# Dense products ahead of TensorE's first wait in eight stages, and score products on quarters of the array in a local attention

## The reference, cut to what matters

```
DIM = 128; HEADS = 8; DIM_HEAD = 64; WINDOW = 64; QK_SCALE = 8.0
def local_attention(q, k, v):
    b, h, n, d = q.shape
    w = n // WINDOW
    bq = q.reshape(b, h, w, WINDOW, d) * QK_SCALE
    bk = k.reshape(b, h, w, WINDOW, d)
    bv = v.reshape(b, h, w, WINDOW, d)
    bk, bv = (look_around(bk), look_around(bv))
    sim = jnp.einsum('bhwid,bhwjd->bhwij', bq, bk)
    mask = (i < j) | (i > j + WINDOW) | (j == -1)
    sim = jnp.where(mask, -jnp.finfo(sim.dtype).max, sim)
    attn = jax.nn.softmax(sim, axis=-1)
    out = jnp.einsum('bhwij,bhwjd->bhwid', attn, bv)
    return out.reshape(b, h, n, d)
...
o = local_attention(q, k, v)
x = x + o @ wo
```

## Time and profile before

| | us |
|---|---|
| median of 3 runs | 4181.39 |
| lowest and highest of them | 4177.72, 4183.64 |
| profiled execution, its own time | 4167.43 |
| its span, first to last instruction | 4165.7 |

### The profile page before, as it was taken

One profiled execution on the slowest core, in us unless ns is written; L12 is line 12 of the kernel. 1 busy time (PEld: TensorE's weight loads), 2 busy tenths in 40 slices (PEclk: granted clock), 3 DMA queues, 4 the chain that ended last, 5 costly groups with the idle time before them and its releaser, 6 DMA issues. The chain is left out here.

```text
span 4165.7 us, 87048 instructions
## 1 busy us (share of the span) xinstructions
PE 3015.8 (72%) x34526; PEld 2091.1 (50%) x34526; DVE 2557.0 (61%) x7026; ACT 1448.0 (35%) x2873; POOL 787.8 (19%) x759
## 2 busy tenths in 40 slices
PE   4567887886547788788554778878856477787885
PEld 3434565654434456565443445656535244565653
DVE  6674565557676456555757745764575764566457
ACT  4134433422404344342240434434224044343421
POOL 3132211101213221110121322121012132111110
PEclk7579999997657899899765889999976588999996
DMA  1011000000001100000000110000000011000000
GB/s 37 6 38 30 14 3 2 14 20 1 7 6 38 30 14 3 2 14 20 1 7 6 40 30 12 3 2 18 16 1 7 6 40 30 11 3 2 19 14 6
DMA packets 65264, 59.65 MB, mean 14 GB/s; under 512 B 16403, under 2 KB 54212, under 8 KB 64838
## 3 DMA queue, kind: packets, MB, share of 16 engines
q1 hardware_dynamic: 63606, 53.24, 4.7%
q10 hardware_dynamic: 1232, 0.61, 0.1%
HBM read 36.29 MB, written 2.10 MB: 9 GB/s over the span
## 5 line engine op out<-in xcount | busy, mean ns | idle before, releaser
L157 POOL TENSOR_TENSOR ln_rstd<-ln_var_eps,neghalf 128x4 f32<-128x4 f32 x128 | 130.1, 1017 | 1223.6 <-DVE ln_var_eps L169 1188.5
L1188 POOL TENSOR_TENSOR l1t_ss<-l1t_ss,neghalf 128x16 f32<-128x16 f32 x64 | 243.7, 3808 | 478.8 <-DVE l1t_ss L1222 478.8
L2103 ACT ACTIVATE l2r_P<-l2r_bank_score 128x512 f32<-128x512 f32 x320 | 173.7, 594 | 176.3 <-PE l2r_bank_score L1825 176.3
L2103 ACT ACTIVATE l2a_P<-l2a_bank_score 128x512 f32<-128x512 f32 x320 | 173.7, 594 | 168.7 <-PE l2a_bank_score L1825 168.7
L1395 PE MATMUL l1t_ring<-l1f_qkv,x_normT 128*128 128x512 f32 x384 | 218.8, 699 | 13.1 <-ACT x_normT L1095 13.1
L1995 DVE CUSTOM_DVE_ANT_0 l2r_masked<-l2r_bank_ring,l2r_neg_wide 128x512 bf16<-128x512 f32 (+1 forms) x256 | 148.7, 622 | 76.7 <-PE l2r_bank_ring L1794 76.4
L1995 DVE CUSTOM_DVE_ANT_0 l2a_masked<-l2a_bank_ring,l2a_neg_wide 128x512 bf16<-128x512 f32 (+1 forms) x256 | 149.0, 622 | 73.9 <-PE l2a_bank_ring L1794 72.6
L1825 PE MATMUL l2a_bank_score<-l2a_q_head,l2a_k_head 32*128 32x128 f32 x2560 | 188.3, 284 | 2.4 <-DMA l2a_q_head<-l2a_shiftT 1.0
L1794 PE MATMUL l2r_bank_ring<-l2r_k_head,l2r_q_head 32*128 32x128 f32 x2432 | 174.6, 286 | 19.9 <-DVE l2r_m L1995 9.8
L1794 PE MATMUL l2a_bank_ring<-l2a_k_head,l2a_q_head 32*128 32x128 f32 x2432 | 176.7, 286 | 16.4 <-DVE l2a_m L1995 7.1
L1825 PE MATMUL l2r_bank_score<-l2r_q_head,l2r_k_head 32*128 32x128 f32 x2560 | 186.0, 282 | 2.6 <-DMA l2r_q_head<-l2r_shiftT 1.2
(11 more groups left out here) (616 smaller groups left out, 7949.6 us busy)
## 6 DMA issues: line engine op xcount, KB each, us to landing
l1t_v_low<-l1t_v SPq DMA_DIRECT2D x112, 130.0 KB, 2.3
l2e_w<-in_L_ffn_w SPq DMA_DIRECT2D x96, 128.0 KB, 2.3
l1f_qkv<-in_L_ffn_wqkv SPq DMA_DIRECT2D x8, 768.0 KB, 4.5
l1f_tables<-in_l_tables SPq DMA_DIRECT2D x8, 512.0 KB, 6.0
l1f_w<-in_L_ffn_w SPq DMA_DIRECT2D x8, 341.0 KB
x_in<-in_L_attn_hidden_states SPq DMA_DIRECT2D x10, 256.0 KB, 3.5
l1f_wo<-in_L_ffn_wo SPq DMA_DIRECT2D x8, 256.0 KB, 4.8
l2a_q_head<-l2a_shiftT SPq DMA_DIRECT2D x128, 2.0 KB
```

The source lines that it names most:

```text
L157: pool.tensor_tensor(b.rs[:, p, :], b.ve[:, p, :], b.neghalf[:, 0:NT], ALU.pow).then_inc(s["post_rstd"] if post else s["pre_rstd"], 1)
L1188: pool.tensor_tensor(ss[:, n % 2], ss[:, n % 2], b.neghalf[:, 0:2 * H8], ALU.pow).then_inc(s["rn_ready"], 1)
L2103: act.activation(self.P[:, use % self.P_RING].rearrange("k h q -> k (h q)"), self.score_bank(h, g)[:, :], ACT.Exp, scale=self.scale).then_ ...
```

## The change

**Dense products.** A new function `busy` issues `count` bfloat16 products of 128x512, the identity times a mask, into a bank that the stage overwrites later. It stands as the first thing in TensorE's program in eight blocks, ahead of `transpose_x` and its wait: 20 in l0_ffn, 10 in l1_attn, 10 in the local attention at depth 0, 10 in l2_attn, 20 in l2_ffn_attention, 10 in the experts, 10 in l3_attn, 20 in l3_ffn. They feed nothing.

**Score products.** `scores(n)` now writes the masks and then 24 q·k products: for each chunk, the 64 keys of the tile's first block against all 128 queries, into partitions 0 to 63 of the bank; the 64 keys of the block before against the first 64 queries and those of the second block against the last 64, into partitions 64 to 127. So each product uses 64 rows and 64 columns of the array. The order of keys in the banks changes with it: `neg_k` is built anew, and the two halves of `v_low` change places. For the first tile of a sequence POOL clears the upper half of `v_low` instead of the lower, with a settle before and after.

**Order.** The products with the shift are a function of their own, `subtract(n)`, with the wait for L1338 ahead. `scores(n + 1)` is issued after the projection of v and before `turn_output(n - 1)`, and no longer waits for the shift.

The programs of VectorE, ScalarE and SP keep their order.

```
+def busy(pe, b, bank, count):
+    for _ in range(count):
+        pe.matmul(bank[:, :], b.ident_bf[:], b.neg["row_gt"][:].unsqueeze(1).to_broadcast([128, 4, 128]),
+                  start=True, stop=True)
...
+            busy(pe, b, y[1], 20)                      # l0_ffn
             transpose_x(pe, b, s["xq_ready"], s["xT_psum"], xq, bank)
...
+            busy(pe, b, at.ring[0], 20)                # l2_ffn_attention
             transpose_x(pe, b, s["h_ready"], s["hT_psum"], h, at.y)
...
     for first, m in enumerate(w.neg_k):
-        keep(m[:], [[0, 2], [-1, 64]], 0, 1, fill=MASKED)
-        keep(m[:], [[0, 2], [1, 64]], 64, -1, fill=MASKED)
-        if first:
-            keep(m[:, 0:64], [[0, 64]], -64, 1, fill=MASKED)
+        keep(m[:, 64:128], [[-1, 64]], 0, 1, fill=MASKED)
+        keep(m[:, 64:128], [[1, 64]], 64, -1, fill=MASKED)
+        keep(m[:, 0:64], [[1, 64]], 0, -1, fill=MASKED)
+        if not first:
+            own.settle()
+            own(pool.tensor_copy(m[64:128, 0:64], w.neg_low[64:128, 0:64]))
...
-                sync.dma_start(v_low[64:128, p, j], v[0:64, p, j]).then_inc(s["v_low_ready"], 16)
+                sync.dma_start(v_low[0:64, p, j], v[0:64, p, j]).then_inc(s["v_low_ready"], 16)
                 if j:
-                    sync.dma_start(v_low[0:64, p, j], v[64:128, p, j - 1]).then_inc(s["v_low_ready"], 16)
+                    sync.dma_start(v_low[64:128, p, j], v[64:128, p, j - 1]).then_inc(s["v_low_ready"], 16)
...
-            own(pool.memset(v_low[0:64, :, 0], 0.0))
+            own.settle()
+            own(pool.memset(v_low[64:128, :, 0], 0.0))
+            own.settle()
...
             def scores(n):
                 j, p = tiles[n]
-                pe.wait_ge(s["q_ready"], n + 1)
-                pe.wait_ge(s["k_ready"], n + 1)
-                pe.wait_ge(s["shiftT_ready"], n + 1)
                 if n:
                     pe.wait_ge(s["p_ready"], 2 * n)
...
+                pe.wait_ge(s["q_ready"], n + 1)
+                pe.wait_ge(s["k_ready"], n + 1)
+                for c in range(CHUNKS):
+                    at = 128 * c
+                    for half, here, keys, queries in ((0, 0, j * 128 + 64, slice(0, 128)), (1, 0, j * 128, slice(0, 64)),
+                                                      (1, 64, j * 128 + 128, slice(64, 128))):
+                        for u in range(2):
+                            rows = slice(64 * u, 64 * u + 64)
+                            pe.matmul(s_bank[u][64 * half:64 * half + 64, at + here:at + queries.stop],
+                                      k[rows, p, c, keys:keys + 64], q[rows, n % 2, c, queries], start=False, stop=True,
+                                      skip_group_check=True)
+
+            def subtract(n):
+                p = tiles[n][1]
+                pe.wait_ge(s["shiftT_ready"], n + 1)
                 for u in range(2):
                     for c in range(CHUNKS):
-                        pe.matmul(s_bank[u][:, c * 128:(c + 1) * 128], w.sel[:, 4 * u + c, :], shiftT[:, p, :],
-                                  start=False, stop=True, skip_group_check=True)
...
+                        last = pe.matmul(s_bank[u][:, c * 128:(c + 1) * 128], w.sel[:, 4 * u + c, :], shiftT[:, p, :],
+                                         start=False, stop=True, skip_group_check=True)
+                    last.then_inc(s["s_ready"], 1)
...
+            scores(0)
             turn_shift(0)
             for n in range(T):
-                scores(n)
+                subtract(n)
...
                 if n + 3 < T:
                     project(n + 3, "v")
+                if n + 1 < T:
+                    scores(n + 1)
                 if n:
                     turn_output(n - 1)
```

More of the change, by code:

```diff
@@ L965, in _ @@
         def _(pe):
+            busy(pe, b, k_ps[0], 10)
             transpose_x(pe, b, s["xn_ready"], s["xT_psum"], b.xn, y)
@@ L1031, in l1_ffn_constants @@
         own(pool.tensor_copy(m[64:128, :], w.neg_low[64:128, :]))
+    own.settle()
+    own(pool.memset(w.neg_low[:], 0.0))
+    keep(w.neg_low[:, 0:64], [[-1, 64]], -64, 1, fill=MASKED)
     for first, m in enumerate(w.neg_k):
-        keep(m[:], [[0, 2], [-1, 64]], 0, 1, fill=MASKED)
-        keep(m[:], [[0, 2], [1, 64]], 64, -1, fill=MASKED)
-        if first:
-            keep(m[:, 0:64], [[0, 64]], -64, 1, fill=MASKED)
+        keep(m[:, 64:128], [[-1, 64]], 0, 1, fill=MASKED)
[4 more added lines that the diff above has]
+            own(pool.tensor_copy(m[64:128, 0:64], w.neg_low[64:128, 0:64]))
     keep(w.sel[:], [[-1, H8], [0, 128]], 0, 1, ALU.not_equal, 1.0)
@@ L1374, in _ @@
             if d == 0:
+                busy(pe, b, y[1], 10)
                 transpose_x(pe, b, s["xn_ready"], s["xT_psum"], b.xn, y)
@@ L1475, in scores @@
                               start=True, stop=True, skip_group_check=True)
+                pe.wait_ge(s["q_ready"], n + 1)
[12 more added lines that the diff above has]
+                pe.wait_ge(s["shiftT_ready"], n + 1)
                 for u in range(2):
                     for c in range(CHUNKS):
-                        pe.matmul(s_bank[u][:, c * 128:(c + 1) * 128], w.sel[:, 4 * u + c, :], shiftT[:, p, :],
-                                  start=False, stop=True, skip_group_check=True)
-                for c in range(CHUNKS):
-                    for blk in range(2):
-                        keys, at = j * 128 + 64 * blk, 128 * c + 64 * blk
-                        for u in range(2):
-                            rows = slice(64 * u, 64 * u + 64)
-                            last = pe.matmul(s_bank[u][:, at:at + 64], k[rows, p, c, keys:keys + 128],
-                                             q[rows, n % 2, c, 64 * blk:64 * blk + 64], start=False, stop=True,
-                                             skip_group_check=True)
-                            if (c, blk) == (CHUNKS - 1, 1):
-                                last.then_inc(s["s_ready"], 1)
+                        last = pe.matmul(s_bank[u][:, c * 128:(c + 1) * 128], w.sel[:, 4 * u + c, :], shiftT[:, p, :],
+                                         start=False, stop=True, skip_group_check=True)
+                    last.then_inc(s["s_ready"], 1)
             project(0)
@@ L2489, in _ @@
         def _(pe):
+            busy(pe, b, out[0], 10)
             transpose_x(pe, b, s["t_ready"], s["xT_psum"], t, turned)
@@ L2713, in _ @@
         def _(pe):
+            busy(pe, b, ring[3], 10)
             transpose_x(pe, b, s["xn_ready"], s["xT_psum"], b.xn, ring)
@@ L2921, in _ @@
         def _(pe):
+            busy(pe, b, g_ps[0], 20)
             transpose_x(pe, b, s["xq_ready"], s["xT_psum"], xq, t_ps)
```

## The result

The changed kernel takes 4054.5 us (median of 4 runs, 4051.5 to 4056.6). Beside it the kernel before takes 4182.5 us (4177.7 to 4191.5). The ratio is 0.969, with a 95% interval from 0.967 to 0.971. The forecast was 4118, with a range from 4075 to 4158: the direction was right, and the gain was twice the one forecast.

What follows compares the result with a forecast made beforehand. TensorE was taken to bound the local attention. Score products -47, order -15, clock +14 and dense products -15 sum to -63 us: 4104 for the profiled run, 4118 as median, range 4075 to 4158.

Steps and rivals of the forecast that it cites:

- What bounds: Local attention tile: TensorE sets the time, so each nanosecond it saves counts until VectorE's 2.58 us of slack is gone.
- The score products: q·k in each local attention tile: 1.93 us falls to 1.2, saving 47 us over 64 tiles (37 to 68).
- the ends 0.87 to 1.35: Bounds in us for a tile's q·k: 0.87 if quarters never idle, 1.35 at the pace of the values' records.
- The maxima's row: Profile row of sixteen bfloat16 records on four quarters, 22 ns each; at that rate 48 records take 1.05 us.
- The float32 row: Profile row of the values' float32 products on array halves, records 28 ns apart; at that rate 48 take 1.35 us.
- The place in the order: Local attention: issuing the next tile's scores earlier fills no wait in steady tiles, only at pass starts: 15 us (8 to 18).
- The starts of the passes: First two tiles of each local attention pass: earlier scores fill waits, 1.9 us for each of eight passes, 15 us.
- The clock in the local attention: More clock falls expected in the eight passes, 3.5 us each: 14 us more than now (14 less to 36 more).
- The stage starts: Dense products ahead of stages' first waits raise the clock for real products: 15 us gained (0 to 30).
- The step from the profile to the median: Whole kernel: the median before lies 14 us above the profiled run, so 4104 becomes a forecast median of 4118.
- the second, no loss of clock: Rival for the local attention: clock falls stay or vanish and l2_ffn_attention is always warm; 4063 to 4098 us, chance 0.22.
- the strict order: Rival for q·k: records start only in program order, 1.7 us a tile, gain 15 us, total 4150; chance 0.13.

## Why the prediction was wrong

By its own steps:

- **What bounds.** Right. Each 0.1 us that TensorE lost in a tile came off the pass, and VectorE's slack was not used up: in the tile shown it still idles for 2.1 of 10.92 us.
- **The score products.** 1.10 us, inside the ends 0.87 to 1.35 and below the 1.2 taken. I had averaged two rows. The maxima's row, of the same shape of tile, gave 22 ns a record; the new ones take 1.10 / 48 = 23 ns. The float32 row, on halves, was the wrong one to average in. 54 us instead of 47.
- **The place in the order.** "Moving it saves nothing unless it fills a wait" failed. The move changed what stands behind the wait, and 0.26 of its 0.56 us was the restart and not ScalarE; 0.20 of that went. 64 x 0.20 = 13 us that the sum did not have. The row that shows it was in the trace of before: the copy of the shift ends 0.26 us ahead of the mask. The starts of the passes were right: about 2 us each, 17 in all, for the 15 forecast.
- **The clock in the local attention.** Forecast 14 us more, measured about none. Steady terms give 54 + 13 + 17 = 84, and the two depths gained 83.6. The falls inside passes went from five to seven, but at some 1.6 us each where they had cost 2.8: in depth 1, two falls took 107.0 - 103.9 = 3.1 us. The forecast of more falls was right and its price was not: I gave each of the eight passes 3.5 us, from the old falls, and two of those had kept the clock low for 10 us at a time, as here in turn 2 of the kernel before:

```profile
1305.00:1314.00 9.00, 9.00 (x52) 6.95 (x52) 3.98 (x6) 3.82 (x7) 3.81 (x1) 0.50 0.04 9
```

The larger price of the clock, at the beginning of a pass, was in none of my terms; it did not make the forecast wrong, since the change left it there.
- **The stage starts.** 15 us forecast, 28 measured. Right: l0_ffn and l3_ffn next to nothing at 20 products, l1_attn 0.8 for nothing, l2_attn 4.3 for 6, though unevenly (1.7 us in turns 1 and 4, 0.4 in turns 2 and 3). Mis-sized: l3_attn, 2.7 us a turn for the 0.75 forecast. The earlier rise is worth 1.4 us, the difference between the two turns without a second fall (59.9 before, 58.5 after). The rest is that second fall, some 19 us into the stage. It came in three turns of four before and cost 2.5 to 3.1 us, and in two after, at 1.8. Wrong in its reason: l2_ffn_attention gained the whole 9 us, and it does so without its dense products too. That this term came out at all is luck: the trace of before happened to hold one slow turn, the second one two.
- **The step from the profile to the median.** The trace of before was 14 us better than its median, that of after was not. This is 17 us of the 128. The kernel before spreads over 4155 to 4193 in all its runs here, the four runs of the changed one over 5 us: a profile of before is one draw among several courses of the clock.

The miss of 64 us is so made up of 13 (restart), 7 (q·k), 2 (starts), 14 (clock), 13 (stages) and 17 (the draw), less 2 of rounding and small stages.

The rival nearest to the result was the second, no loss of clock, at 4063 to 4098 with a chance of 0.22. Even it lacked the restart.

## What to carry to other kernels

Look at what stands behind a wait: the time between the releaser's end and the waiting engine's first instruction is a cost of its own, and here 0.11 of its 0.26 us went by swapping two waits. Dense products in a wait helped here where they lasted until the real work came (in l3_attn they end 0.1 us ahead of it); those that ended 3.1 us (l2_ffn_attention) or 6.3 us (l0_ffn) ahead of it gave their stages nothing that the runs show. And a gain in one stage of a kernel whose clock rises and falls has to be read stage by stage, from more than one profile, since stages that an edit did not touch changed by up to 10 us.

## What the runs showed of the hardware

- A busy TensorE did not by itself have the full clock. In l2_ffn_attention the profile has it busy for 22.96 of 23.00 us at 0.50. The Trainium skill (TensorE: Matmul & The Clock Gate, Part 1: The HAM clock gate) says that activity releases the clock. This trace disagrees if "activity" is read as a busy engine, and the prediction called the trace in agreement beside a row that was not: 13.00 of 13.00 us at 0.50.
- Float32 products on four quarters of the array follow one another at 23 ns, as the bfloat16 ones did at 22, and not in the strict order that would have made it 1.7 us for a tile. The same page (Part 3: Packing small matmuls) says that matmuls start strictly in program order; the first records of the products, as far as they can be told apart, keep to it, and the 1.10 us disagree with that rule applied to the two records of one float32 product.
- A wait that was already fulfilled cost TensorE 0.11 us behind one that it had just waited for (0.56 to 0.45 us by swapping the two).
